# GpSimd adds the two halves of the squared gated rows, and TensorE sums them with one product in place of two

## What is computed

```
y = y * (z * jax.nn.sigmoid(z))                              # 256 values per token
y = y * jax.lax.rsqrt(jnp.mean(y * y, -1, keepdims=True) + EPS) * rms_w
out = y @ W_out.T                                            # 256 -> 128
return x + out
```

## Time and profile before

| | us |
|---|---|
| median of 3 runs | 794.11 (792.69 to 797.33) |
| the profiled execution | 795.79 |
| its span, first to last instruction | 794.0 |
| PE busy in the span | 631.2 (79%) |
| DVE busy | 585.2 (74%) |
| ACT busy | 462.3 (58%) |
| POOL busy | 400.4 (50%) |

### The profile page before, as it was taken

One profiled execution on the slowest core, in us unless ns is written; L12 is line 12 of the kernel. 1 busy time (PEld: TensorE's weight loads), 2 busy tenths in 40 slices (PEclk: granted clock), 3 DMA queues, 4 the chain that ended last, 5 costly groups with the idle time before them and its releaser, 6 DMA issues. The chain is left out here.

```text
span 794.0 us, 15139 instructions
## 1 busy us (share of the span) xinstructions
PE 631.2 (79%) x3701; PEld 531.9 (67%) x3703; DVE 585.2 (74%) x1410; ACT 462.3 (58%) x1014; POOL 400.4 (50%) x601
## 2 busy tenths in 40 slices
PE   0695629998999989999998998699898889988700
PEld 0695317777778777778777776587777777777600
DVE  7787898898898888888898888555565555654445
ACT  0352446688777878877788775454555555554400
POOL 3000006576766766766676767145555555555510
PEclk9999999799999999999999999799999999999955
DMA  9950100000000000000000015133333333333169
GB/s 306 266 130 0 29 1 23 19 27 23 29 22 22 28 22 22 28 22 22 25 26 22 29 24 184 36 88 99 97 85 96 88 98 98 85 98 86 54 252 382
DMA packets 64647, 61.43 MB, mean 77 GB/s; under 512 B 9242, under 2 KB 55710, under 8 KB 64624
## 3 DMA queue, kind: packets, MB, share of 16 engines
q1 hardware_dynamic: 56176, 44.11, 19.7%
q0 software_dynamic: 8448, 17.06, 6.2%
HBM read 30.19 MB, written 31.47 MB: 78 GB/s over the span
## 5 line engine op out<-in xcount | busy, mean ns | idle before, releaser
L449 POOL DMA_INDIRECT moe_d<-raw,slot_st x136 | 133.8, 984 | 124.6 <-issue 102.1
L422 POOL DMA_INDIRECT slots_d<-rows,slot_st x128 | 134.6, 1052 | 73.8 <-POOL rows L417 52.5
L1040 DVE SCALAR_TENSOR_TENSOR act<-raw,taps,act 128x512 f32<-128x512 f32 x192 | 149.3, 785 | 23.9 <-ACT act L513 23.1
L398 POOL TENSOR_TENSOR xde<-xb,e_end 128x256 f32<-128x256 f32 x64 | 45.6, 713 | 113.2 <-DVE xb L1117 111.6
L1233 DVE CAST x_hi<-bank 128x256 fp32r<-128x256 f32 x68 | 28.8, 424 | 95.4 <-PE bank L871 91.8
L864 PE MATMUL bank<-xw_hi,x_hi 128*128 x136 | 61.1, 449 | 27.2 <-DVE x_lo L1235 22.7
L774 PE MATMUL bank<-xb,m_sb 128*128 128x64 f32 x512 | 75.9, 298 | 3.8 <-POOL xde L398 3.8
L774 PEld LDWEIGHTS bank<-xb,m_sb 128*128 128x128 f32 x512 | 73.1, 216 | 5.6 <-issue 3.9
L890 PE MATMUL bank<-act,raw 128*128 x544 | 72.0, 275 | 1.8 <-issue 1.8
L664 ACT ACTIVATE raw<-bank 128x256 f32<-128x256 f32 x68 | 26.5, 391 | 77.2 <-remote 68.5
L890 PEld LDWEIGHTS bank<-act,raw 128*128 128x128 f32 x544 | 66.1, 192 | 1.9 <-issue 1.9
(11 more groups left out here) (231 smaller groups left out, 1659.4 us busy)
## 6 DMA issues: line engine op xcount, KB each, us to landing
slots_d<-rows SPq DMA_DIRECT2D x8, 1122.0 KB, 13.4
rows<-slots_d SPq DMA_DIRECT2D x68, 132.0 KB
x_sb<-in_x SPq DMA_DIRECT2D x8, 512.0 KB, 7.0
act<-in_x SPq DMA_DIRECT2D x64, 64.0 KB
xw_hi<-moe_d SPq DMA_DIRECT2D x8, 512.0 KB, 9.3
xw_lo<-moe_d SPq DMA_DIRECT2D x8, 512.0 KB, 9.9
out<-x_sb SPq DMA_DIRECT2D x8, 512.0 KB, 13.5
moe_d<-raw,slot_st POOLq DMA_INDIRECT x136
```

Source lines behind the costliest of these rows:

```text
L398: nc.gpsimd.tensor_tensor(by_head(xde[:, u, :]), by_head(xdt[:, u, :]), per_head(e_end, nn), ALU.mult).then_inc(xde_done, 1)
L422: nc.gpsimd.indirect_dma_start(out=slots_d, out_offset=bass.IndirectOffsetOnAxis(ap=slot_st[:, r, c:c + 1], axis=0), in_=rows[:, r, c, :], ...
L449: nc.gpsimd.indirect_dma_start(out=moe_d, out_offset=bass.IndirectOffsetOnAxis(ap=slot_st[:, r, c:c + 1], axis=0), in_=ym[r][:, c * D:(c + ...
L1040: V.scalar_tensor_tensor(out=group_act(par)[:, t, :], in0=proj[:, t, k:k + GT], scalar=taps[:, t, k:k + 1], in1=group_act(par)[:, t, :], o ...
```

## The change

`square` stays as it is. GpSimd adds the second half of `sq` to the first, in place, 128 by 128 in fp32, at the end of each step, behind `xde`; `project_out` waits for that addition (`sq_sum`) in place of ScalarE's square, and makes one product with the ones column in place of two. Two additions follow behind the last step.

```
+        sq_sum = sem("sq_sum")
...
+            def add_halves(nn, u):
+
+                pool.wait_ge(sq_done, nn + 1)
+                nc.gpsimd.tensor_tensor(sq[:, u, 0:P], sq[:, u, 0:P], sq[:, u, P:2 * P], ALU.add).then_inc(sq_sum, 1)
+
             def sequence(b):
...
                     if not (is_last(b) and j == SC - 1):
                         inputs_to_end(nn + 1, (j + 1) % 2)
+                    if not (is_first(b) and j < 2):
+                        add_halves(nn - 2, j % 2)
 
             inputs_to_end(0, 0)
             over_sequences(pool, sequence)
+            add_halves(NT - 2, 0)
+            add_halves(NT - 1, 1)
...
             def project_out(nn, u, early):
-                pe.wait_ge(sq_done, nn + 1)
+                pe.wait_ge(sq_sum, nn + 1)
                 if not early:
                     pe.wait_ge(o_kept, nn)
                 for c in range(2):
                     mm(bank[7][:, 0:D], yg[:, u, c * P:(c + 1) * P], wo_sb[:, c, :], start=(c == 0), stop=(c == 1))
-                for c in range(2):
-                    m = mm(bank[7][:, D:D + 1], sq[:, u, c * P:(c + 1) * P], ones[:, 0:1], start=(c == 0),
-                           stop=(c == 1))
-                m.then_inc(o_done, 1)
+                mm(bank[7][:, D:D + 1], sq[:, u, 0:P], ones[:, 0:1], start=True, stop=True).then_inc(o_done, 1)
```

## The result

The changed kernel takes 818.8 us in the median of 4 runs (812.43 to 823.28), the one before 795.01: ratio 1.0283, 95% interval 1.0242 to 1.0323. It is slower, well above the forecast (796.2) and outside its range (785.5 to 805). The profiled execution takes 815.81 us with a span of 814.1, 20.1 us longer than before.

What follows compares the result with a forecast made beforehand. The prediction took a loop of about 24 us over TensorE, ScalarE and VectorE as the bound. Terms -2.8 + 0 + 1.9 + 1.0 + 2.0 = +2.1 us on the 794.11 median gave 796.2 us, range 785.5 to 805.

Steps and rivals of the forecast that it cites:

- one product less: TensorE's second sum-of-squares product removed, 0.2 us a tile; one of four counted in 14 groups, 2.8 us gained.
- rival A: Mixer loop: three of the four product removals in a group land, -6.4 us, 787.7 us; chance 0.22.
- The addition lies within its bounds: GpSimd's fp32 addition of 128 x 128: 0.33 us taken, bounds 0.28 to 0.61 us.
- The step on TensorE's clock: Mixer loop: more idle ahead of the SiLU wait loses one of three full-clock groups, +1 us.
- All three lost would be +3: Upper bound of the clock term: all three full-clock groups of the loop lost, 0.9 us each, +3 us.
- The addition against VectorE: q = 2 step: delayed `state_k` meets VectorE's taps in a third of 14 groups, 0.4 us each, +1.9 us.
- rival B: q = 2 step: addition pushes `state_k` and row copy onto VectorE's taps in every group, +7.8 us, 801.9; chance 0.28.
- The end of the stage: Last mixer steps: six additions of 0.33 us ahead of the last `xde`, +2.0 us, bounds 1.7 and 3.7.
- I count 0 for both: `project_out` at q = 2 and q = 3: the sum is ready in time or covered by the SiLU wait, 0 us.

Runs made afterwards that it cites:

- the relay: Kernel before, plus GpSimd adding only one of 128 columns, TensorE waiting for that, both products kept: 806.9 us; 790.2 with unread products in TensorE's waits.
- filling: Unread bf16 products of 128 x 512 put into TensorE's q = 3 waits: kernel before 785.1 us (2 and 4 products), changed kernel 799.9 (7 and 2).
- The one-product kernel: Kernel before without the second half of the sum of squares, no GpSimd addition: 810.4 us; 784.8 with filling.
- the filled kernel: Kernel before with 2 unread products ahead of `project_out` at q = 3 and 4 behind it: 785.1 us, ratio 0.9858.
- The write-only run: Changed kernel with filling, GpSimd's addition replaced by a memset of 128 x 320 with no SBUF input, TensorE waiting for it: 798.4 us, ratio 1.0022.
- the addition beside: Kernel before plus a GpSimd addition of two constant tiles that nobody waits for, both products kept: 813.4 us; 797.0 with filling.

## Why the prediction was wrong, by its own steps

The sum as forecast, and as measured. Since the batches had runs of the kernel before of their own, the measured terms are differences of ratios, times 795 us:

| term | forecast | measured | from |
|---|---|---|---|
| one product less | -2.8 | +0.2 (-0.3 by medians) | 0.9861 - 0.9858 |
| addition, in the loop and at the end (with some clock at the end) | +1.9 + 2.0 | +12.7 | 1.0018 - 0.9858; stages of the profiled executions +7.7 and +4.6 |
| wait for the sum | 0 | +1.7 (+2.9 by medians) | 1.0040 - 1.0018 |
| clock | +1.0 | +8.0 | (1.0283 - 1.0040) - (1 - 0.9858) |
| sum | +2.1 | +22.5 | 1.0283 - 1 |

The third row holds the product's removal too, so the sum is that of rows two to four, without the first. Its two kernels have intervals of 0.2 and 0.3%, so the wait for the sum is -1 to 5 us. The split between rows two and three hangs on the order in which the parts are added: by way of the relay the wait, with 0.2 us of addition, comes first and costs 8.6 us, and the length of the addition then 5.9.

*What held.* The reading that TensorE is not the bound of the loop, although 93% busy, was right, more than I gave it credit for: removal brought nothing that the runs can tell, where I counted 2.8 us, and rival A (787.7) fell. The addition lies within its bounds.

*The step on TensorE's clock failed most,* by 7 of the 20 us that the sum is short: +1.0 forecast, +8.0 measured. "All three lost would be +3" took the groups of before for the worst that can be: 23.8 us at 0.93. Even of those it priced the milder kind: six of the 13 took 24.2 to 24.3 us, and filling brings these to 22.9 as well, so they lost 1.3 and not 0.9. The runs show that more idle time at q = 3 takes groups to 0.82 and 25.8 to 27.1 us, a cost of 3 to 4 us each and not 0.9. The direction stood in the text ("less work makes TensorE idle longer ahead of that wait"); its price was cut off at what the trace of before happened to hold. The one-product kernel shows the size without any other edit: 15 us, and none of it with filling. At the end of the stage, where the forecast counted no clock at all, it fell from 0.89 to 0.72; what that costs is in the other rows.

*The addition against VectorE failed by size.* The term was 1.9 us; measured 7.7. I counted one meeting in three at 0.4 us. The loop of the filled kernel grew by 7.7 us, 0.6 in each of 13 groups, more than the upper bound of 5.6. The mechanism was rival B's, the shift of `state_k` and its like onto VectorE's instructions, which I had at 0.28; its price was too low, since it looked at the q = 2 taps alone and the gate pays as well (472 to 576 ns), above all at q = 3, where `state_k` used to end 0.05 us ahead of it. The write-only run is the evidence that the shift, and not the addition's own reads, does most of it. By the Trainium skill's rule at its strictest the term would have been 8.4; measured 7.7. That is nearer than mine, though the mechanism in it, each meeting at the whole length of `state_k`, was not shown to be what makes up the 7.7.

*The end of the stage* was a count of six additions at 0.33. In the kernel with the addition beside it costs 4.6, and 0.47 x 6 = 2.8 of it would be the additions; the rest goes with the long GpSimd rows beside `xw_lo`, a line which I had not looked for in those steps, and with a clock of 0.81 in place of 0.88. How it divides between the two was not measured. In the changed kernel, filled, the end costs 7.5.

*"I count 0 for both" in the wait for the sum* failed. The cover was the SiLU, and it was worked out from one group with `xde` at 307.82 and the addition at 308.2. After, the step itself is later: TensorE waits 1.84 us for the sum at q = 3 and still 0.49 for the SiLU. In the loop that is mostly cover taken over, and its price is the clock; beside that every second group is 0.5 us longer at full clock (23.9 against 23.4 with the addition beside). At the end there is no cover. TensorE waits 8.6 us for the sum there in five waits, where it had waited 3.8 for `xde`, the longest being:

```profile
514.59 0.71 PE L803 MATMUL bank<-wo_sb,yg 128*128 128x128 f32 x4 [2.65 <-POOL sq L430]
```

From the addition beside to the changed kernel, both filled, the loop grows from 330.1 to 332.3 us and the end from 38.4 to 41.4, 5.2 together; the medians give 2.9 and the ratios 1.7, so the size of this term is known only roughly.

*What stays open.* Why the losses by the clock, each less the 11.3 us of the kernel before (14.8 for the product alone, 2.7 for the addition, 2.0 for the relay, 8.0 for the whole), don't add up isn't resolved: from run to run the changed kernel itself varies by 11 us, with the mean granted clock (812.43 at 0.925, 823.28 at 0.904). Nor did a run part the meetings with the taps from those with the gate, or the clock at the end of the stage from the waits there.

## What to carry to other kernels

Ask of an engine's work whether the path that closes the loop goes through it before you take any off; here 12.8 us off TensorE (by the estimate) were worth nothing measurable. When TensorE is as full as here and waits in one place of each group, treat a change that lengthens this wait as one that may cost the clock for the next groups, 1 to 2% here, and try a few unread products in the wait: two a group made the kernel before about 1.2% faster. Before an operation goes to GpSimd, list what stands behind it in its order and which VectorE instructions those will now meet.

## What the runs showed of the hardware that I had not expected

- Less work made the kernel slower: one product of 0.2 us less a tile, 810.4 against 795.4 us.
- Unread products made it faster: 785.1 against 795.9 us, with six a group; the same kind at another place raised the clock as well (0.950 to 0.965 in place of 0.927 to 0.947) but lengthened the groups, 793.3 against 793.9.
- An fp32 addition of 128 x 128 on GpSimd takes 0.47 us in the mean of the loop and 1.45 beside one VectorE instruction with two SBUF inputs of 128 x 1024.
- The slow groups are slow by more than their wait: 3.9 us longer at a mean clock of 0.82 where TensorE idles 2.4 us a group in place of 1.7.
